# A recurrence begun after three instead of six warming matmuls, with two wide zero matmuls between its first nine steps, the large loads held back, and the last tile's GELU layer in halves on two engines

## The reference, cut to what matters

```
h_t = tanh(h_{t-1} @ Wh + x_t @ Wx + b),  t = 0..127, h_{-1} = cond      # recurrence, 8 rows wide
w, idx = gate(h @ Wg.T)            # sigmoid, best 2 of 4 groups, best 4 of 16 experts, scaled to 2.5
x1 = x + sum_e we_e * ((silu(h @ W1[e].T + b1[e]) * (h @ W3[e].T + b3[e])) @ W2[e].T + b2[e])
o  = ((x1 * cond/sqrt(128)) @ Wc) * demod
hp = bitlinear(o, F1) + fb1        # 128 -> 512; ternary weights, 8-bit tokens (scale = row maximum / 127)
out = x1 + bitlinear(gelu(hp), F2) + fb2                                   # 512 -> 128
```

## Time and profile before

| | |
|---|---|
| three executions | 147.68 us median (146.3 to 149.26) |
| the profiled execution | 145.98 us, span of its instructions 144.2 us |
| mean granted TensorE clock | 0.999 |
| TensorE busy | 139.8 us (97%) |
| VectorE busy | 104.0 us (72%) |
| ScalarE busy | 82.9 us (58%) |
| GpSimd busy | 33.7 us (23%) |
| DMA | 13.90 MB, mean 96 GB/s |

### The profile page before, as it was taken

The page is one execution under the profiler, slowest core; times in us unless marked ns, Lnnn a source line. Parts: engine busy times, 40 slices in busy tenths (PEclk is TensorE's granted clock), DMA queues, the critical chain, the costliest instruction groups (busy, mean ns, idle before and its releaser), DMA issues.

```text
span 144.2 us, 3607 instructions
## 1 busy us (share of the span) xinstructions
PE 139.8 (97%) x1149; PEld 131.8 (91%) x1149; DVE 104.0 (72%) x399; ACT 82.9 (58%) x277; POOL 33.7 (23%) x86
## 2 busy tenths in 40 slices
PE   6999999999999999999999999999999999999993
PEld 2598899999999999999999999999999987999992
DVE  4300298989987688529999537999785999799741
ACT  3022366577874355545565554489858614869871
POOL 3000047299905460000151000006110002301100
PEclk9999999999999999999999999999999999999999
DMA  4999200270035000088000059200006910000111
GB/s 78 374 379 380 98 0 0 55 241 6 0 113 182 6 2 5 5 259 324 6 0 0 2 123 368 100 0 0 5 5 149 402 40 0 18 0 7 39 52 36
DMA packets 6693, 13.90 MB, mean 96 GB/s; under 512 B 1586, under 2 KB 3219, under 8 KB 6291
## 3 DMA queue, kind: packets, MB, share of 16 engines
q1 hardware_dynamic: 6384, 13.61, 28.5%
q10 hardware_dynamic: 290, 0.07, 0.2%
HBM read 13.08 MB, written 0.59 MB: 95 GB/s over the span
## 4 chain that ended last, share of the span: by engine, by line
PE 84%; DVE 7%; issue 3%; DMA 3%; ACTq 1%; DVEq 0%; ACT 0%
PE a L1048 19%; PE b L1048 17%; PE y_ps L1157 13%; PE rnn L1089 9%; PE y_ps L1060 8%; DVE hid L978 3%; DMA h_sb<-h0T 3%; PE b L1157 2%; DVE hid L969 2%; PE m_ps L1089 2%; PE a L1184 2%; PE y_ps L1152 1%; PE rnn L1163 1%; PE rnn L1036 1%; PE m_ps L1107 1%
## 5 line engine op out<-in xcount | busy, mean ns | idle before, releaser
L969 DVE SCALAR_TENSOR_TENSOR hid<-b,b_sb,gate_u 128x256 f32<-128x256 f32 (+1 forms) x80 | 33.7, 424 | 11.5 <-PE b L1048 5.8
L741 ACT ACTIVATE hs<-rnn 128x8 f32<-128x8 f32 x112 | 19.8, 177 | 33.0 <-PE rnn L1089 30.6
L1089 PEld LDWEIGHTS rnn<-hs,wh_sb 128*128 128x128 f32 x224 | 34.8, 191 | 0.8
L765 ACT ACTIVATE gate_u<-a,b_sb 128x256 f32<-128x256 f32 (+1 forms) x80 | 33.5, 427 | 3.1 <-DVE hid L969 1.9
L1157 PE MATMUL y_ps<-hid,w_sb 128*128 128x128 f32 (+1 forms) x160 | 32.6, 321 | 0.0
L1089 PE MATMUL rnn<-hs,wh_sb 128*128 128x8 f32 x224 | 32.6, 218 | 0.0
L978 DVE TENSOR_TENSOR hid<-hid,we_bc 128x128 f32<-128x128 f32 (+1 forms) x80 | 24.7, 349 | 0.7 <-DMA we_bc<-we_dram 0.7
L1157 PEld LDWEIGHTS y_ps<-hid,w_sb 128*128 128x128 f32 x160 | 24.2, 191 | 1.0
L1060 PE MATMUL y_ps<-warm_sb 128*128 128x256 bf16 x108 | 16.8, 271 | 0.0
L1048 PE MATMUL a<-hs_hi,w_lo 128*128 128x256 f32 x48 | 16.4, 341 | 0.0
L1048 PE MATMUL a<-hs_hi,w_hi 128*128 128x256 f32 x48 | 15.2, 316 | 0.0
(11 more groups left out here) (152 smaller groups left out, 269.4 us busy)
## 6 DMA issues: line engine op xcount, KB each, us to landing
we_bc<-we_dram SPq DMA_DIRECT2D x12, 512.0 KB, 5.8
we_bc<-we_dram SPq DMA_DIRECT2D x8, 256.0 KB, 4.5
w_sb<-W1T SPq DMA_DIRECT2D x1, 1024.0 KB, 6.1
w_sb<-W3T SPq DMA_DIRECT2D x1, 1024.0 KB, 8.4
w_sb<-W2T SPq DMA_DIRECT2D x1, 1024.0 KB, 7.7
out<-out_sb SPq DMA_DIRECT2D x8, 64.0 KB, 1.5
xT_sb<-xT SPq DMA_DIRECT2D x1, 448.0 KB, 4.0
f_sb<-F1T SPq DMA_DIRECT2D x1, 256.0 KB, 6.1
```

Of the source, the lines that this page charges most:

```text
L741: act.activation(hs[:, cols], rnn_bank(n * BATCH, BATCH), ACT.Tanh).then_inc(h_ready, 1)
L765: act.activation(gate_u[:, n % U_RING, 0:w], a_ps[n % 2][:, 0:w], ACT.Silu, bias=b1_sb[:, e:e + 1]).then_inc(silu_ready, 1)
L969: dve.scalar_tensor_tensor(out=hid[:, n % H_RING, 0:w], in0=b_ps[n % 2][:, 0:w], scalar=b3_sb[:, e:e + 1], in1=gate_u[:, n % U_RING, 0:w], ...
L1089: pe.matmul(rnn_bank(n * BATCH, BATCH), wh_sb[:], prev, start=False, stop=True, skip_group_check=True).then_inc(z_ready, 1)
```

## The change

- `START_KEEPS` is 3 instead of 6. Behind each of the steps 0 to 8 two zero matmuls of 128x512 (`WARM`) are put, and steps 1 to 9 stand behind them in TensorE's order. `KEEP` is placed only after the last `WARM`. The small bias matmul (`BIAS`) that the seeds need moves behind step 2.
- SyncE waits until `Wx`, tile 0 of `x`, `Wh` and `h0` have landed before it issues the 448 KB of `x`, W1 and W3; and until W1 and W3 have landed before it issues the second layer's operands, F1, F2 and W2.
- For the last tile (`LAST` = 7): `HP_READ`, `GELU` and `AMAX2` go in two halves of 256 columns, where the first half's maximum is put in column 513 of `hp` and the second reduction takes it in; `ROUND2` and `T2_READ` have their first half on ScalarE and their second on VectorE; the transposes of the second half go to the bank `m_ps`.
- `T2_READ` of tile 0 is on VectorE. `XT` of tile 6 stands behind `T2` of tile 3.
- The scheduler's constants are others: `PE_SLIP` 0.07 instead of 0.27, `ACT_SLIP` 0.03 instead of 0, `MARGIN` 0.05 instead of 0.13, and all of `LIFT`. So the order differs on all engines. `weighted_on_dve` is rewritten with the same outcome.

```diff
+READ2_ON_DVE = (0,)
+LAST = TILES - 1
-START_KEEPS = 6
+START_KEEPS = 3
+WARM_STEPS = 9
...
-PE_SLIP, ACT_SLIP, KEEP_SLIP, MARGIN = 0.27, 0, 0.09, 0.13
+PE_SLIP, ACT_SLIP, KEEP_SLIP, MARGIN = 0.07, 0.03, 0.09, 0.05
...
+TURNS = [(("XT", 6), ("T2", 3))]
...
+    put("PE", "BIAS", 0, [(0.14, 0.007), (0.12, 0.007)], RESULT, [], [("RNN", 2)])
+    for k in range(2 * WARM_STEPS):
+        put("PE", "WARM", k, [(LOAD, 0.213)], RESULT, [], [("RNN", k // 2)] + same("WARM", k))
     for t in range(STEPS):
         behind = same("RNN", t)
+        if 0 < t <= WARM_STEPS:
+            behind.append(("WARM", 2 * t - 1))
...
             sp.dma_start(wx_sb[:], Wx).then_inc(xw_in, 16)
             sp.dma_start(wh_sb[:], Wh).then_inc(rnn_in, 16)
+            sp.wait_ge(xw_in, 32)
+            sp.wait_ge(rnn_in, 32)
             sp.dma_start(xT_sb[:, P:TOKENS], xT[:, P:TOKENS]).then_inc(x_in, 16)
...
             sp.dma_start(wg_sb[:], WgT).then_inc(gate_in, 16)
+            sp.wait_ge(moe_in, 32)
             sp.dma_start(cond_sb[:], condT).then_inc(l1_in, 16)
...
+                if kind == "GELU_FIRST":
+                    act.wait_ge(hp_first, 1)
+                    act.activation(hp[:, n, FIRST], hp[:, n, FIRST], ACT.Gelu).then_inc(gelu_first, 1)
...
+                if kind == "AMAX2_FIRST":
+                    dve.wait_ge(gelu_first, 1)
+                    mark(dve.tensor_reduce(hp[:, n, MAXIMUM], hp[:, n, FIRST], AX_X, ALU.max, apply_absolute_value=True), (kind, n))
+                if kind == "ROUND2_B":
+                    dve.wait_ge(inv2_ready, n + 1)
+                    dve.tensor_scalar(hp[:, n, SECOND], hp[:, n, SECOND], inv_step[:, 2 * n + 1:2 * n + 2], MAGIC,
+                                      ALU.mult, ALU.add).then_inc(rounded2_b, 1)
+                if kind == "T2_READ_B":
+                    wait_filled(dve, "T2_B", n)
+                    dve.tensor_scalar(q2T[:, n % 2, SECOND], m_ps[:, FIRST], MAGIC, None, ALU.subtract).then_inc(freed[M], 1)
...
             for kind, n in ORDERS["PE"]:
+                if kind == "WARM":
+                    keep_wide()
```

More of the change, by code:

```diff
@@ L147, in put @@
     def put(self, engine, kind, n, length, seen, after=(), behind=(), table=None):
-        self.ops[(kind, n)] = (engine, length, seen, list(after), list(behind), table)
+        self.ops[(kind, n)] = (engine, length, seen, list(after), list(behind) + [b for a, b in TURNS if a == (kind, n)], table)
     def ranks(self, followers):
@@ L416, in build_orders @@
         put("PE", "HP", i, [(0.06, 0.213)], RESULT + 0.05, [("Q_READ", i)] + late("HP"), same("HP", i))
-        put("DVE", "HP_READ", i, 0.66, 0.80, [("HP", i), ("DEQ1", i)], same("HP_READ", i))
-        batch = next(b for b in GELU_BATCHES if i in b)
-        put("ACT", "GELU", i, 0.54, 0.69, [("HP_READ", k) for k in batch] + [("TANH", STEPS - 1)], same("GELU", i), "gelu")
-        put("DVE", "AMAX2", i, 0.60, 0.74, [("GELU", i)], same("AMAX2", i))
+        if i == LAST:
+            put("DVE", "HP_FIRST", i, 0.36, 0.50, [("HP", i), ("DEQ1", i)])
+            put("DVE", "HP_READ", i, 0.36, 0.50, [("HP", i), ("DEQ1", i)], same("HP_READ", i) + [("HP_FIRST", i)])
+        else:
+            put("DVE", "HP_READ", i, 0.66, 0.80, [("HP", i), ("DEQ1", i)], same("HP_READ", i))
+        batch = next(b for b in GELU_BATCHES if i in b)
+        ready = [("HP_READ", k) for k in batch] + [("TANH", STEPS - 1)]
+        if i == LAST:
+            put("ACT", "GELU_FIRST", i, 0.33, 0.48, [("HP_FIRST", i)], same("GELU", i), "gelu")
+            put("ACT", "GELU", i, 0.33, 0.48, ready, [("GELU_FIRST", i)], "gelu")
+            put("DVE", "AMAX2_FIRST", i, 0.33, 0.47, [("GELU_FIRST", i)], same("AMAX2", i))
+            put("DVE", "AMAX2", i, 0.33, 0.47, [("GELU", i), ("AMAX2_FIRST", i)])
+        else:
+            put("ACT", "GELU", i, 0.54, 0.69, ready, same("GELU", i), "gelu")
+            put("DVE", "AMAX2", i, 0.60, 0.74, [("GELU", i)], same("AMAX2", i))
         put("DVE", "SCALE2", i, 0.065, 0.20, [("AMAX2", i)], same("SCALE2", i))
@@ L423, in build_orders @@
         put("POOL", "DEQ2", i, 0.25, 0.35, [("SCALE2", i)], same("DEQ2", i))
[L424 to L427, removed]
+        half = i == LAST
+        put("ACT", "ROUND2", i, 0.40 if half else 0.71, 0.56 if half else 0.86, [("RECIP2", i)], same("ROUND2", i))
+        put("PE", "T2", i, [(LOAD, 0.107)] * (2 if half else 4), RESULT + 0.05, [("ROUND2", i)] + late("T2"),
+            same("T2", i) + two_ago("OUT"))
+        behind = same("T2_READ", i) if i and read2_on_dve(i) == read2_on_dve(i - 1) else []
+        if read2_on_dve(i):
+            put("DVE", "T2_READ", i, 0.60, 0.74, [("T2", i)], behind)
+        else:
+            put("ACT", "T2_READ", i, 0.33 if half else 0.58, 0.50 if half else 0.75, [("T2", i)], behind)
+        if half:
+            put("DVE", "ROUND2_B", i, 0.30, 0.44, [("RECIP2", i)])
+            put("PE", "T2_B", i, [(LOAD, 0.107)] * 2, RESULT + 0.05, [("ROUND2_B", i)], [("T2", i)])
+            put("DVE", "T2_READ_B", i, 0.30, 0.44, [("T2_B", i)])
+        put("PE", "OUT", i, [(0.06, 0.06)] * 4, RESULT + 0.05, [("T2_READ", i), ("XB", i)] + [("T2_READ_B", i)] * half, same("OUT", i))
         put("DVE", "OUT_READ", i, 0.27, 0.41, [("OUT", i), ("DEQ2", i), ("XB", i)], same("OUT_READ", i))
@@ L1077, in _ @@
             for kind, n in ORDERS["PE"]:
+                if kind == "WARM":
+                    keep_wide()
+                if kind == "BIAS":
+                    pe.matmul(a_ps[0][:, 0:1], bh_row[:], ones_row[:, 0:1], start=True, stop=True, skip_group_check=True).then_inc(marked, 1)
                 if kind == "XIN":
@@ L1182, in _ @@
                     wait_free(pe, kind, n)
-                    for k in range(HB):
+                    for k in range(HB // 2 if n == LAST else HB):
                         last = pe.transpose(banks[b][:, k * P:(k + 1) * P], hp[:, n, k * P:(k + 1) * P], ident[:])
                     last.then_inc(filled[b], 1)
+                if kind == "T2_B":
+                    pe.wait_ge(rounded2_b, 1)
+                    wait_free(pe, kind, n)
+                    for k in range(HB // 2):
+                        at = HIDDEN // 2 + k * P
+                        last = pe.transpose(m_ps[:, k * P:(k + 1) * P], hp[:, n, at:at + P], ident[:])
+                    last.then_inc(filled[M], 1)
                 if kind == "OUT":
```

65 lines of the change are left out of this document (46 added, 19 removed), and 10 rows, old and new, of the table LIFT.

## The result

The changed kernel takes 147.95 us median (146.66 to 149.86, 20 executions), the kernel before 147.76 us in executions beside them (145.57 to 149.88, 20). The ratio is 1.0097, 95% interval 1.0059 to 1.0135: less than 2% slower, but clear of no change. The profiled execution takes 147.69 us against 145.98, its span 145.9 against 144.2. The forecast was a median of 145.0, and a profiled execution 2.0 us shorter than before.

The account below looks back on a forecast made before the run. Bounds: the recurrence in the head, TensorE's work in the middle, the last tile's VectorE and ScalarE chain in the tail. -0.6 - 0.2 - 1.2 = -2.0 us: 144.0 profiled, 145.0 median; range takes in 142.6 and 148.2.

Parts of the forecast that it names:

- the head: Stage up to the first expert matmul: earlier step 0 and two low-clock steps together -0.6 us, bounds -1.6 to +6.4.
- two is my value: Head: two recurrence steps would run at the low clock, which would rise at about 6.5 us; +1.0 us.
- The price of a step: Head: a step at the low clock takes 1.1 to 1.2 us against 0.655, so 0.5 us lost for each.
- Step 0: Head: the recurrence's first step would start at 4.3 us instead of 5.88, -1.6 us, with 0.9 for bias and input products.
- the covers of the held transfers: Head: delayed loads still land before use, W3 at 13.6 us with 2.7 us cover; all at nothing.
- I take -0.2: Middle, about 17 to 131 us: better order against the smaller slip's holes; -0.2 us, bounds -1.0 to +1.5.
- the reordering takes what the tail gives: Rival: holes or collisions of 1.5 to 2 us over the 112 steps, sum -0.3 to 0, 146.8 us; chance 0.13.
- The tail: After the last Y product: last tile's halves -0.97, shorter wait before `ROUND1` -0.2; -1.2 us, bounds -1.8 to -0.3.
- the halves waiting for ScalarE's read of an earlier tile: Tail, sign of being wrong: the last tile's halves wait for ScalarE's reads of tiles 5 and 6.
- steps over 1 us apart beyond the fourth: Head, sign of being wrong: recurrence steps stay over 1 us apart beyond the fourth.
- the low clock stays: Rival, first sixteen steps: 0.5 us per low step, gain of 3.0 used up at six, +5.0 at sixteen; chance 0.13.
- `h0` no earlier: Rival, head: the 4 KB load is slow by itself, step 0 at 5.9 us; +0.1, 147 us; chance 0.08.

Follow-up runs that it names:

- e7: The kernel before with SyncE's waits and three wide zero matmuls ahead instead of six, none wide between the steps; 147.83 us median, ratio 1.0034.
- e9: e8 with the change's start: three wide zero matmuls ahead, two behind each of steps 0 to 8, bias and input products behind them; 147.32 us, ratio 1.0028.
- e1: The kernel before with only the two waits on SyncE's queue added; 147.57 us median, ratio 0.9973.
- e8: The kernel before with SyncE's waits and the last tile's halves, old start and old constants; 145.60 us median, ratio 0.9908.
- e4: The kernel before with only the last tile's halves added; 147.33 us median, ratio 0.9969.
- e3: The changed kernel with the old PE_SLIP, ACT_SLIP, MARGIN and LIFT; 150.73 us median, ratio 1.0161.
- e10: e8 with eight wide zero matmuls ahead instead of six; 146.15 us median, ratio 0.9964.
- e6: The kernel before with the new LIFT and its own slips and margin; 151.60 us median, ratio 1.0270.

## Why the prediction was wrong

Two steps of the prediction failed about equally: the head came out 1.7 us worse than forecast (+1.1 for -0.6), the middle 1.8 (+1.6 for -0.2).

**In the head it is "two is my value" for the steps at the low clock.** It was two steps at 0.5, +1.0; measured were five at 0.44, less in the last, +2.0. The price of a step was right, their number was not. I reasoned that the clock would rise soon because TensorE isn't idle in between. In the profiled execution it rose at about 10, five us after step 0, in e7 and e9 at about 10.3 and 7.8. And it isn't only a matter of broken streaming: e1 and e8 have one head, and the trace of one is low until 9.4, with six wide matmuls ahead, and of the other high before 4.8. What sets the moment stays open.

The rule of the Trainium skill beside it ("TensorE: Matmul & The Clock Gate", Part 1: the same kernel is released after a number of matmuls that differs from run to run) agrees with these two traces. I had kept it as a remark, and not as a term for the kernel before, and so took that kernel's profiled execution, with a rise at 4.1, for the usual one.

Its group holds a third of the executions (35 of 101). The comparison is then not of an early start against a safe one. Begun early, the recurrence had three to five slow steps in each profile (after, e7, e9); begun after six wide matmuls, it had none in the profiles of the fastest groups (before, e4, e8), and that the early start has given up. Nor do the changed kernel's 20 executions reach under 146.66 us, while 8 of the 20 before do. This is also why the medians differ by 0.2 us only and the profiled executions by 1.7.

**Step 0** came to 4.85, not 4.3: the bias product started at 3.54 and the input product at 4.27, both at the low level with nothing else between. The two took 1.3 us up to step 0, where I had put 0.9. So it was -1.0 instead of -1.6. The loads behave as forecast, and the covers of the held transfers held (W3 at 12.1 against the first expert matmul at 18.05).

**The middle** is the largest single miss: taken at -0.2 with +1.5 as the bound, it came to +1.6. The step that failed is "I take -0.2", with the order's cost bounded by holes in the steps' slots alone. e3 shows that the constants are the cause (114.27 with the old ones). What they did is only in part what I had in mind: stops of 0.55 us more, the largest with VectorE held beside GpSimd and a product waiting; about 0.6 us net of second-layer work drawn ahead of the last sum; the remaining 0.4 or so is open. The rival "the reordering takes what the tail gives" had the right price, 1.5 to 2 us, at a chance of 0.13. What should have been weighed is that all ranks of a list that ran nearly without holes were replaced.

**The tail** was right in size: -1.04 for -1.2, but a part of it is work moved ahead of the mark. Its parts: the halves 0.62 (e4) for 0.97, since GELU won nothing there (0.41 a half was better than my 0.47, but ScalarE was busy); the order 0.42 for 0.2. One of my signs of being wrong came here, the halves waiting for ScalarE's read of an earlier tile (138.72), and one in the head, steps over 1 us apart beyond the fourth.

**The rivals.** The one on the slower side, the low clock stays, was the mechanism at less than its full length: that the gain is used up at six low steps was right as a price, and with the middle's loss on top five were enough. `h0` no earlier is refuted (1.9 us instead of 4.1). As a whole: -0.6 -0.2 -1.2 became +1.1 +1.6 -1.0. The median of 147.95 lies inside the range by luck of its width; the direction does not.

## What to carry to other kernels

Before a start is moved, look at several executions: if the times lie in groups, the profile shows one of them, and the groups may be the thing to change. Zeros ahead of a serial chain cost their own time once (0.8 us for two more in e10); a chain begun at the low clock pays for every step until the clock rises (0.44 us each here). When a list of operations is re-ranked together with other edits, run the re-ranking alone and the edits alone: here two of the edits gained 0.9% (e8), and the new start and the re-ranking hid it. And when a stage is measured between two marks, count the work between them: a new order can move work across a mark.

## What was unexpected of the hardware

- With the same instructions ahead of it the clock reached its high level before 4.8 us in one execution (e8) and at about 9.4 in another (e1), which moved the completion of tile 0 by 2.0 us.
- After 1.04 us without a matmul, ending at 7.05, the granted clock read 1.00 from 6 to 8 us and 0.52 from 8 to 10 (e6).
- A 4 KB load took 4.1 to 5.3 us in five profiles with 448 KB and 1 MB loads issued around it, and 1.8 to 2.3 in nine with these held back.
- At the start of the traces the granted clock's column reads 1.00 where matmuls of 512 columns take 634 ns and not 380; the duration is what shows the level there.
- A 128x8 scaling on VectorE took 1.23 us beside the second of two 128x512 subtractions on GpSimd, and ended when that did; before, without one beside it, it took 0.16.
